# An adaptive layer of attention and a recurrent net: the last four sequences' path in two halves, one base sum on VectorE, later constants, new queue orders

## What is computed

```python
y = jnp.einsum('bnh,boh->bno', x, weight[subject_id]) + bias[subject_id][:, None, :]
sim = jnp.einsum('bhid,bhjd->bhij', q, k) / sqrt(hd) / (abs(temperature)[0] + 0.1)
for fi, freq in enumerate([31., 37., 41., 43., 47.]):
    scores = scores + alpha[:, fi] * jnp.sin(TWO_PI * sim / freq + phi[:, fi])
w = jax.nn.sigmoid(scores); w = w / (sum(w, -1) + 1e-10)
out = layernorm((w @ v) @ Wo.T + bo) * gamma + beta;  x = x + out
h = relu(x @ W1[language] + b1[language]);  a = x + h @ W2[language] + b2[language]
z = layernorm(a) * gamma[language] + beta[language]
def step(c, xt):                       # the scan runs over the 32 sequences
    f, i = sigmoid(xt @ wf.T + c @ uf.T + bf), sigmoid(xt @ wi.T + c @ ui.T + bi)
    return f * c + i * tanh(xt @ wc.T + c @ uc.T + bc)
result = x + tanh(z @ wo.T + c_final @ uo.T + bo)
```

## Time and profile before

| | us |
|---|---|
| median of 3 runs | 320.94 (320.41 to 322.8) |
| the profiled execution | 323.39 |
| its span | 321.6 |
| TensorE matmul busy | 285.4 (89%) |
| VectorE busy | 274.6 (85%) |
| ScalarE busy | 257.3 (80%) |
| GpSimd busy | 51.6 (16%) |

### The profile page before, as it was taken

How to read it: one execution, slowest core, us unless ns; L and a number is a source line. 1 busy time by engine, 2 the same in 40 slices (tenths; PEclk the granted TensorE clock), 3 DMA queues, 4 the chain that set the end, 5 groups by cost and what they waited for, 6 DMA issues and landing times.

```text
span 321.6 us, 7374 instructions
## 1 busy us (share of the span) xinstructions
PE 285.4 (89%) x2686; PEld 177.5 (55%) x2686; DVE 274.6 (85%) x598; ACT 257.3 (80%) x378; POOL 51.6 (16%) x58
## 2 busy tenths in 40 slices
PE   0787898969889989999999998899999999998971
PEld 0576647866546855554575645556665545543350
DVE  3049996999999999999999998999999998554265
ACT  1069998999999999999999999899999894422132
POOL 5000600041100012332100214140013331210000
PEclk9999997998999999999999999999999999999997
DMA  5698427544044248045445240330444160020007
GB/s 174 244 388 303 93 30 227 116 135 67 0 91 117 30 113 242 0 75 118 103 88 143 74 68 1 71 70 15 108 106 67 35 150 16 2 34 2 0 0 261
DMA packets 32374, 31.97 MB, mean 99 GB/s; under 512 B 10706, under 2 KB 24274, under 8 KB 32338
## 3 DMA queue, kind: packets, MB, share of 16 engines
q1 hardware_dynamic: 27410, 26.67, 29.1%
q0 software_dynamic: 4352, 4.20, 8.7%
q10 hardware_dynamic: 576, 0.64, 0.8%
HBM read 23.36 MB, written 2.10 MB: 79 GB/s over the span
## 4 chain that ended last, share of the span: by engine, by line
DVE 39%; PE 32%; ACT 14%; issue 8%; DMA 3%; POOL 2%; SPq 1%; DVEq 0%; ACTq 0%; POOLq 0%
DVE sc L1626 12%; PE pg L694 7%; DVE ang L1615 5%; PE pg L685 5%; DVE ang L1606 5%; ACT ang L1130 4%; PE pf L491 3%; PE pav L589 3%; ACT ang L1139 3%; PE pf L571 2%; PE pf L547 2%; DVE fc L1761 2%; ACT sc L1121 2%; DMA w<-x 1%; DVE vz L1596 1%
## 5 line engine op out<-in xcount | busy, mean ns | idle before, releaser
L1139 ACT ACTIVATE ang<-ang,qs 128x2560 f32<-128x2560 int32 x32 | 77.4, 2433 | 0.3 <-DVE ang L1615 0.2
L1626 DVE SCALAR_TENSOR_TENSOR sc<-ang,ratio,sc 128x512 f32<-128x512 f32 (+1 forms) x120 | 73.0, 637 | 0.4
L1130 ACT ACTIVATE ang<-sc,phase 128x512 int32<-128x512 f32 (+1 forms) x110 | 64.5, 650 | 0.0
L685 PE MATMUL pg<-gate_w,zT 128*64 128x384 f32 x256 | 50.8, 499 | 0.6 <-DVE zT L1751 0.4
L694 PE MATMUL pg<-gate_u,cT 128*64 128x384 f32 x256 | 47.7, 493 | 1.6 <-DVE cT L1770 1.5
L1615 DVE TENSOR_SCALAR ang<-ang 128x2560 int32<-128x2560 int32 x32 | 47.5, 1501 | 0.0
L1606 DVE TENSOR_SCALAR ang<-sc,phase 128x256 int32<-128x256 f32 (+1 forms) x90 | 32.4, 412 | 2.6 <-ACT sc L1121 2.5
L1179 ACT ACTIVATE gat<-pg 128x384 f32<-128x384 f32 x32 | 15.6, 487 | 22.7 <-PE pg L694 22.3
L694 PEld LDWEIGHTS pg<-gate_u,cT 128*64 128x64 f32 x256 | 16.4, 136 | 22.1 <-issue 15.0
L513 PE MATMUL pf<-wc,xg 128*64 128x256 f32 x128 | 17.1, 416 | 9.5 <-DMA wc<-in_cond 8.8
L1149 ACT ACTIVATE sc<-sc,lead 128x512 f32<-128x512 f32 (+1 forms) x40 | 23.4, 628 | 2.3 <-DVE sc L1626 2.2
(11 more groups left out here) (114 smaller groups left out, 474.1 us busy)
## 6 DMA issues: line engine op xcount, KB each, us to landing
wc<-in_cond SPq DMA_DIRECT2D x30, 257.0 KB, 3.5
w<-in_up SPq DMA_DIRECT2D x32, 128.5 KB, 2.6
wa<-in_down SPq DMA_DIRECT2D x32, 66.0 KB, 1.9
xt<-in_xt SPq DMA_DIRECT2D x8, 256.0 KB, 3.0
xt<-rows POOLq DMA_DIRECT2D x8, 256.0 KB, 4.2
w<-x POOLq DMA_DIRECT2D x8, 256.0 KB, 4.2
xg<-in_x SPq DMA_DIRECT2D x3, 512.0 KB, 5.1
qm<-qT SPq DMA_DIRECT2D x48, 32.0 KB, 2.1
```

Of the source, the lines that this page charges most:

```text
L685: pe.matmul(pg[n % 2][u * L:(u + 1) * L, 0:GCOLS], zT[:, q % 2, kc, t * L:(t + 1) * L], gate_w[:, kc, u, :], start=False, stop=(kc == KC - ...
L1130: op = act.activation(ang[:, n % SLOTS, f, r], unit(n)[:, r], ACT.Identity, scale=TURN / FREQS[f], bias=phase[:, p * NF + f:p * NF + f + 1])
L1139: act.activation(a.bitcast(F32), a, ACT.Sin, scale=2 * PI_LOW / TURN, bias=qs[:, 3:4]).then_inc(sine_ready, 1)
L1626: op = dve.scalar_tensor_tensor(out=unit(n)[:, r], in0=ang[:, n % SLOTS, f, r].bitcast(F32), scalar=ratio[:, p * NF + f:p * NF + f + 1], i ...
```

## The change

Six things. The chain of part 7 is cut into two halves j, one tile of 128 tokens each, with calls of their own (..._half), in the two banks of pf, which the groups' scores and values have left; normalised halves go to ytok. input_gates of steps 28 and 29 wait for half 0 of zT, 30 and 31 for half 1. Part 7's base is a sum by VectorE (base_half), no DMA. The rows of parts 6 and 7 come from TensorE; biases of steps 13, 21 and 28 move to TensorE, those of 17 and 24 to ScalarE; angles 10/3, 12/3 and 21/2 go to VectorE, 22/1 to ScalarE. Since part 7 leaves pr, keep_output_part(5) can wait: it stands between the tanhs of the end, and output_part(7) waits for it. The constants of later layers are loaded behind the first weights of group 1. And the lists of all engines are put in a new order; each list has the same calls as before but for those named, and for the number of warm matmuls (dummy work on pct). The orders are cut here to the start and the last part; in between, steps 3 to 7 of the recurrence stand earlier in each list, queries(3, 1), keys(3, 1) and scores(10), (11) later, queries(4, 1), keys(4, 1) and copy_scores(28) earlier, centre_output_weights far earlier, residual(0) and residual(4) later; SP issues load_rest(0, 1) to (0, 3) behind load_cond(2, ...), and GpSimd's shifted(1) stands ahead of deviation_out(0).

```diff
-ON_ACT = [1, 2, 3, 1, 3, 4, 1, 4, 3, 4, 2, 4, 2, 3, 3, 4, 3, 4, 3, 3, 3, 3, 3, 3, 3, 4, 3, 4, 2, 3, 3, 2]
+ON_ACT = [1, 2, 3, 1, 3, 4, 1, 4, 3, 4, 1, 4, 1, 3, 3, 4, 3, 4, 3, 3, 3, 2, 4, 3, 3, 4, 3, 4, 2, 3, 3, 2]
...
-BIAS_BY_PE = (0, 1, 2, 4, 6, 8, 10, 12, 14, 16, 17, 18, 24, 31)
-ROW_BY_PE = (0, 1, 2, 3, 4, 5)
+BIAS_BY_PE = (0, 1, 2, 4, 6, 8, 10, 12, 13, 14, 16, 18, 21, 28, 31)
+ROW_BY_PE = (0, 1, 2, 3, 4, 5, 6)
 SHIFT_BY_DMA = (0, 1, 2, 3, 4, 5, 6, 7)
-BASE_BY_DMA = (0, 1, 2, 3, 4, 5, 6, 7)
+BASE_BY_DMA = (0, 1, 2, 3, 4, 5, 6)
...
+        def half_chunks(j):
+            return pf[:, j, 0:D].rearrange("p (c n) -> p c n", c=KC)
+
+        def half_tile(j):
+            return pf[:, j, 0:D]
+
+        def half_columns(j):
+            return slice(j * P, (j + 1) * P)
...
+            load_attention_consts()
+            load_rest(0, 0)
+            load_cond(1, 0)
+            load_cond(1, 3)
+            load_cond(1, 1)
+            load_x(1)
+            load_cond(1, 2)
             load_rest_consts()
-            load_attention_consts()
-            load_x(1)
-            load_cond(1, 1)
...
-            load_cond(1, 3)
-            load_cond(1, 0)
-            load_cond(1, 2)
-            load_rest(0, 0)
+            spread_q(1, 0)
+            load_x(2)
+            load_cond(2, 0)
+            spread_q(1, 1)
+            load_cond(2, 3)
+            load_rest(1, 0)
+            load_cond(2, 1)
...
+            def turned_half(j):
+
+                if j == 0:
+                    pe.wait_ge(att_ready, FIRST[NG] // 2)
+                    pe.wait_ge(s_copied, B)
+                    pe.wait_ge(v_ready, NG)
+                k = 2 * (NQ - 1) - FIRST[NG - 1] // 2 + j
+                for c in range(KC):
+                    mm = pe.matmul(half_chunks(j)[:, c, :], atq[:, k, c * P:(c + 1) * P], eye[:, :],
+                                   start=(c == 0), stop=True, is_transpose=True, skip_group_check=True)
+                mm.then_inc(last_turned, 1)
+
+            def output_bias_half(j):
+
+                pe.wait_ge(last_copied, j + 1)
+                for c in range(KC):
+                    pe.matmul(half_tile(j)[:, c * P:(c + 1) * P], out_bT[:, c, :], eye[:, :],
+                              start=(c == 0), stop=True, is_transpose=True, skip_group_check=True)
+
+            def output_projection_half(j):
+
+                for kc in range(KC):
+                    mm = pe.matmul(half_tile(j), stage[:, 1, kc, half_columns(j)], wo[:, kc, :],
+                                   start=False, stop=(kc == KC - 1), skip_group_check=True)
+                mm.then_inc(last_projected, 1)
+
...
+            def adapter_down_half(j):
+
+                pe.wait_ge(last_x1_copied, j + 1)
+                pe.wait_ge(rest_loaded[1], NQ // 2 * 32 * PB)
+                for kc in range(KC):
+                    for row, b in halves(j):
+                        mm = pe.matmul(pf[row:row + L, j, 0:L], wa[:, 1, b, kc * A:(kc + 1) * A],
+                                       stage[:, 1, kc, b * L:(b + 1) * L], start=(kc == 0), stop=(kc == KC - 1))
+                mm.then_inc(last_down, 1)
...
-                if t == 0:
+                if q == NQ - 1:
+                    if t % 2 == 0:
+                        pe.wait_ge(last_z, t // 2 + 1)
+                elif t == 0:
...
-                pe.wait_ge(z_ready, q + 1)
+                if q == NQ - 1:
+                    pe.wait_ge(last_z, 2)
+                    pe.wait_ge(go_kept, NQ - 2)
+                else:
...
             state_turned(22)
-            turned(7)
+            turned_half(0)
+            turned_half(1)
             state_gates(23)
             turn_normed(6)
-            output_projection(7, 0)
-            output_projection(7, 1)
+            output_bias_half(0)
+            output_projection_half(0)
+            output_bias_half(1)
+            output_projection_half(1)
             state_turned(23)
-            gate_bias(24)
             input_gates(24, 0)
             input_gates(24, 1)
             state_gates(24)
             input_gates(25, 0)
-            turn_residual(7)
+            turn_residual_half(0)
+            turn_residual_half(1)
             input_gates(25, 1)
             state_turned(24)
-            adapter_down(7)
+            adapter_down_half(0)
+            adapter_down_half(1)
             state_gates(25)
-            adapter_up(7)
             input_gates(26, 0)
+            adapter_up_half(0)
+            adapter_up_half(1)
             state_turned(25)
             input_gates(26, 1)
             state_gates(26)
             input_gates(27, 0)
             input_gates(27, 1)
-            turn_normed(7)
             state_turned(26)
+            gate_bias(28)
+            turn_normed_half(0)
             state_gates(27)
             input_gates(28, 0)
             input_gates(28, 1)
...
             keys(0, 1)
-            angle(1, 3)
-            angle(1, 4)
             copy_scores(2)
             copy_scores(3)
             sines(0, False)
-            first_biases()
-            halved(0)
+            angle(1, 3)
+            angle(1, 4)
             angle(2, 2)
             angle(2, 3)
             angle(2, 4)
...
             sines(1, False)
             sines(2, False)
             queries(1, 0)
-            halved(1)
+            sines(3, False)
             keys(1, 0)
-            sines(3, False)
+            weights(0, True)
             queries(1, 1)
             keys(1, 1)
-            weights(0, True)
             weights(1, False)
+            halved(0)
+            halved(1)
             copy_scores(4)
             copy_scores(5)
...
             weights(31, False)
             gates(22)
-            turned(7)
-            output_row(7)
+            turned_half(0)
             gates(23)
-            squares(7)
+            turned_half(1)
+            squares_half(0)
+            squares_half(1)
             gates(24)
-            residual_turned(7)
+            residual_turned_half(0)
...
             tail_tanhed(2)
+            keep_output_part(5)
             tail_tanhed(3)
...
+            def base_half(j):
+
+                dve.wait_ge(last_x1, j + 1)
+                dve.wait_ge(rest_loaded[1], NQ // 2 * 32 * PB)
+                dve.tensor_tensor(b2[:, 1, j, :], x1[:, 2 * (NQ - 1) + j, :], b2[:, 1, j, :], ALU.add).then_inc(last_base, 1)
...
+            def modulated_half(j):
+
+                dve.wait_ge(last_norm_turned, j + 1)
+                if j == 0:
+                    dve.wait_ge(gate_done, PB * (NQ - 2))
+                    dve.wait_ge(go_done, NQ - 2)
+                dve.tensor_tensor(z_half(j), half_chunks(j).rearrange("p c (b n) -> p c b n", n=L), half_language(j, 0), ALU.mult).then_inc(last_z_part, 1)
...
             conditioned(0)
             mask_queries(0)
+            centre_output_weights()
             angle(0, 0)
             angle(0, 1)
             angle(0, 2)
+            mask_queries(1)
             angle(0, 3)
             angle(1, 0)
-            mask_queries(1)
             angle(1, 1)
+            wrap(0)
...
             normalise(6)
+            modulated(6)
             cell_step(23, 0)
             cell_step(23, 1)
-            modulated(6)
             shifted_language(6)
             state_copy(23)
-            residual(7)
-            residual_added(7)
+            residual_half(0)
+            residual_half(1)
+            residual_added_half(0)
+            residual_added_half(1)
+            base_half(0)
             cell_step(24, 0)
             cell_step(24, 1)
             state_copy(24)
-            hidden(7)
+            hidden_half(0)
+            hidden_half(1)
+            base_half(1)
             cell_step(25, 0)
             cell_step(25, 1)
-            adapted(7)
             state_copy(25)
-            moments(7, 0)
-            moments(7, 1)
-            normalise(7)
+            adapted_half(0)
+            adapted_half(1)
+            moments_half(0, 0)
+            moments_half(1, 0)
+            moments_half(0, 1)
             cell_step(26, 0)
             cell_step(26, 1)
+            normalise_half(0)
             state_copy(26)
-            modulated(7)
-            shifted_language(7)
+            modulated_half(0)
+            moments_half(1, 1)
+            shifted_language_half(0)
             cell_step(27, 0)
             cell_step(27, 1)
+            normalise_half(1)
             state_copy(27)
             cell_step(28, 0)
             cell_step(28, 1)
             state_copy(28)
+            modulated_half(1)
+            shifted_language_half(1)
             cell_step(29, 0)
             cell_step(29, 1)
             state_copy(29)
```

881 lines of the change are left out of this document (475 added, 406 removed).

## The result

| | before | after |
|---|---|---|
| median | 321.9 us (320.4 to 324.1) | 330.1 us (325.4 to 332.2, 4 runs) |
| ratio | | 1.022, 95% interval 1.015 to 1.029 |
| the profiled execution, its span | 323.39, 321.6 | 325.41, 323.6 |

The forecast was 320.2 us with a range to 324.8: the time lies outside it, on the other side of before. Note that the profiled execution of after is its shortest, and that of before was one of its longer ones: the two traces differ by 2 us where the medians differ by 8. Neither trace can be read as typical by itself, and that turned out to be a part of the story. All ratios here leave out executions more than 1.5% above the fastest of their kernel, among them the 332.2 us of after, the profiled execution of e_fill2 and one of 1553 us in d_more.

What follows compares the result with a forecast made beforehand. VectorE, with the least slack of three nearly full engines, was taken to set the full stage's end, TensorE's chain the last part. Terms -1.2 + 0.9 - 0.9 + 0.3 + 0.2 = -0.7 from 320.94 gave 320.2 us, range 316.5 to 324.8.

Steps and rivals of the forecast that it cites:

- Start, -1.2: 22 to 65 us: values(1) starts at 61.6 instead of 62.42 and angle(7, 0) is already done, saving 1.2 us.
- GpSimd's and SP's queues, "I take 0": Full stage: shifted(1) ahead of deviation_out(0) and the later load_rest(0, 3) were taken to cost 0.
- The wait for GpSimd, -0.9: 65 to 268 us: VectorE's one long wait, for GpSimd's inverse deviation ahead of a residual, goes, saving 0.9 us.
- no new wait: Hand-over to group 3: copying ends at 6.55, VectorE arrives at 6.7, so no wait is added, with little to spare.
- Angles, +0.9: 65 to 268 us: VectorE takes net two more angles at 0.44 us each, adding 0.9 us with nothing to hide behind.
- Last part, +0.3: 268 to 291 us: TensorE's order puts state_gates(24) at 277.95 instead of 277.64, adding 0.3 us; halves free nothing on the chain.
- again 0.3 behind before: Before state_gates(27): gate_bias(28) and turn_normed_half(0) leave the transpose at 290.2, still 0.3 us late, nothing added.
- a sign against itself: Last part: state_gates(24) to (28) closer together than before would mean halves took work off TensorE's chain, making the forecast wrong.
- the two biases at 0.3: Last part: the two biases on TensorE cost 0.3 us, kept against 0 by the skill's weight-load measure.
- End, +0.2: 308 us on: output_part(7) starts 1.2 us later behind keep_output_part(5), mostly hidden, adding 0.2 us; bounds 0 and +1.2.
- A: 22 to 268 us: VectorE's idle time falls from 5.8 to 2 us, total 317.0 us; chance 0.32.
- B: Steps 3 to 7: cell_step too early holds VectorE's queue, 0.25 us at each of 20 steps, total 325.2 us; chance 0.18.

Runs made afterwards that it cites:

- e_fill2: d_fill with ten more dummy matmuls on TensorE ahead of input_gates(0, 0); 326.5 us, ratio 1.013.
- d_more: c_norm with four more moves in VectorE's list, putting sums or conditioned(4) ahead of two normalise and two residual calls; 323.9 us, ratio 1.004.
- a_shift3: The changed kernel with GpSimd's shifted(3) put back behind deviation_adapted(2); 325.9 us, ratio 1.011.
- c_load3: The changed kernel with SP's load_rest(3, 0) moved ahead of load_cond(4, 1), GpSimd's list untouched; 325.7 us, ratio 1.010.
- d_fill: The changed kernel with TensorE's output_part(1, 0) done twice, right ahead of state_gates(5); 325.4 us, ratio 1.011.
- c_norm: a_shift3 with VectorE's normalise of parts 0 to 4 one call of sums later (two calls for part 2); 323.7 us, ratio 1.003.
- d_bnorm: The kernel before with VectorE's normalise of parts 0 to 4 one to three calls earlier; 324.3 us, ratio 1.004.
- d_ang: d_more with angles 10/3 and 12/3 back on ScalarE; 325.1 us, ratio 1.009.
- b_halves: The kernel before with only the last part in halves, including part 7's base, its row and the biases of steps 24 and 28; 322.4 us, ratio 1.000.

## Why the prediction was wrong, point by point

**Start, -1.2: 0.** Step that failed: the base of the comparison, values(1) at 62.42. angle(4, 0) came at 52.2 us, 1.9 earlier than forecast, and values(1) at 59.2, 2.4 earlier; both look like a success beyond the forecast, and are none, since the old order without a fall of the clock has its values(1) at 59.3, and the same 23 us behind the conditioned of group 1. The wait of 2.00 us and the clock of 0.96 for the stretch stood in the rows and were taken for properties of the order.

**GpSimd's and SP's queues, "I take 0": some 3.5 us in the median, the largest term.** This is the step that failed most. The forecast followed shifted(1) past deviation_out(0) and load_rest(0, 3) past its conditioning, and both indeed cost nothing. It did not follow the same kind of move one part on, shifted(3) ahead of base(2). The call that was moved is a DMA, and what it waits for is another DMA, which stands in a third list behind a condition of its own. a_shift3 and c_load3 show the price, with the falls that follow from the wait in it.

**A clock that falls: 1.6 us a time, in no step.** The late base made TensorE stand still for 2 us, and the fall came behind that. d_fill has the longer wait for the base and no fall.

**The wait for GpSimd, -0.9 and "no new wait": some +2 by the medians.** The wait at residual(4) went. In its place normalise now stands 1.5 to 2.2 us of work behind the moments, in the five parts of a_shift3, where GpSimd's deviation comes 2.1 to 2.9 us behind them; before, 2.3 to 4.6 us lay between. A residual waits 0.6 us besides. The forecast checked a single hand-over (group 3) and took it for all. c_norm and d_bnorm show 2.2 and 2.0 us in the medians; that d_more, without any of these waits, gains nothing more speaks against a price for each of them.

**Angles, +0.9: not above 0, as far as one run shows.** d_ang has the return of two to ScalarE at +1.2 us. The sum by busy time of the fullest engine fails where the next engine is as full: the term was read off VectorE alone, and ScalarE's 196.32 of 203 us stood beside it.

**Last part, +0.3: -0.35.** Starts of the state matmuls of steps 24 to 27:

```profile
280.45 1.46 PE L780 MATMUL pg<-gate_u,cT 128*64 128x384 f32 x8
284.64 1.46 PE L780 MATMUL pg<-gate_u,cT 128*64 128x384 f32 x8
288.64 1.46 PE L780 MATMUL pg<-gate_u,cT 128*64 128x384 f32 x8
292.28 1.51 PE L780 MATMUL pg<-gate_u,cT 128*64 128x384 f32 x8
```

The last two distances are 4.00 and 3.64 us, and were 4.15 and 3.96. By the tanhs, steps 23 to 24 lost 0.12 us of the 0.3 expected, 25 to 26 gained 0.15 and 26 to 27 gained 0.32: turn_normed_half(0) takes half of what turn_normed(7) took between the transpose and the state matmuls, and the half that the forecast put "again 0.3 behind before" was not behind. So halves did take work off the chain, which the forecast had named as a sign against itself. In the median this gain does not show (b_halves, ratio 1.000). My sum had the two biases at 0.3, and the one step that holds them lost 0.12. By the rule of the Trainium skill (Perfetto Trace Analysis, section Identifying the Most-Contended Engine) the two biases would have cost 0; the trace favours neither.

**End, +0.2: -0.3.** From step 31 to the end of the span after takes 15.4 us, before 15.7. The later output_part(7) was hidden, as said, and where the 0.3 us come from was not traced; the new order of tail_added and tail_residual is the likely place, not shown.

**The rivals.** A (VectorE's idle time falls) was the opposite of what came. B had the direction right, with 325.2 still some 4 us short, and by another mechanism: a list whose head waits, only that the head was an adapted, a normalise and a DMA, and not a cell_step. That 325.2 lies near the profiled execution's 325.41 is luck. Its chance of 0.18 rested on the one hand-over that had been followed.

**What adds up, and what stays open.** By the traces, after stands 6.0 us above before from step 0 to 23 and 0.7 below it behind. Of the 6.0, 1.55 are the wait for the base and 1.65 the fall. The other 2.8 are those of a_shift3, and 2.0 of them lie between step 0 and step 1 alone (15.32 us for 13.36), where VectorE waits 0.2 us only. Counted from the conditioned of group 1, a_shift3 has step 0 0.7 us earlier than b_halves, step 1 1.3 later and step 23 1.5 later; before, with two falls on the way, lies between them at step 23. What in the order makes step 1 late was not tested. The medians differ by 7 to 8 us, more than the profiled executions do. c_norm is still 1.6 us above before, and where that lies was not settled: a_shift3, c_norm and d_more have 174.1 to 174.5 us from step 0 to 23 against 171.5, d_more and d_ang show waits moving rather than going, and the two runs that were to test the middle order failed to isolate it. Nor is it settled how much of c_norm's 2.2 us is the waits: from step 0 on its trace is only 0.2 us shorter than a_shift3's, while the medians differ by 2.2. And the medians of c_load3 and d_fill do not show the 1.1 and 1.8 us by which their traces exceed a_shift3.

## To carry to other kernels

When a diff reorders hand-written queues, list for each DMA that changes place what it waits for, which queue issues that, and what stands behind it; a single call whose data comes late holds a whole list. Compare a trace's milestones with a second execution before subtracting them: a clock fall or a late transfer of 1.6 to 3 us looks like a property of the order. And look for short waits of TensorE behind which the clock falls: dummy matmuls in two of them made the kernel before 0.3% faster (0.4% with the last part in halves), while moving work between three full engines moved only the waits.
